# A fused attention, recurrence and expert kernel: WO and the state update change places in TensorE's order

## What is computed

```
# layer 1: gated linear attention, one token after the other
S = exp(gt)[..., None] * S + kt[..., None] * vt[..., None, :]     # state per head
o = einsum('bhk,bhkv->bhv', qt, S)
o = rms(o, rms_w) * (g * sigmoid(g))
x = x + o @ Wo                                                    # output projection
x = x + gelu(ln(x) @ W1 + b1) @ W2 + b2                           # feed-forward
# layers 2 and 4: softmax router, two of eight experts per token
# layer 3: recurrence
h = tanh(xb_t + h @ A.T)                                          # 1024 steps
y = (hs @ C) @ W_out.T + b_out
```

## Time and profile before

| what | value |
|---|---|
| median of three runs | 1946.68 us |
| the profiled execution's own time | 1937.87 us |
| its span, first to last instruction | 1936.1 us |
| mean granted TensorE clock | 0.961 |
| TensorE matmuls busy | 1796.5 us (93%) |
| TensorE weight loads busy | 1553.0 us (80%) |
| VectorE busy | 1310.4 us (68%) |
| POOL busy | 1121.6 us (58%) |
| ScalarE busy | 917.7 us (47%) |
| DMA engines, queue 1 | 7.8% |

### The profile page before, as it was taken

One profiled execution on the slowest core, in us unless ns is written; L12 is line 12 of the kernel. 1 busy time (PEld: TensorE's weight loads), 2 busy tenths in 40 slices (PEclk: granted clock), 3 DMA queues, 4 the chain that ended last, 5 costly groups with the idle time before them and its releaser, 6 DMA issues.

```text
span 1936.1 us, 47586 instructions
## 1 busy us (share of the span) xinstructions
PE 1796.5 (93%) x16264; PEld 1553.0 (80%) x16264; DVE 1310.4 (68%) x3877; ACT 917.7 (47%) x2534; POOL 1121.6 (58%) x1453
## 2 busy tenths in 40 slices
PE   2588899999999999999999999999999999999887
PEld 1467788888888888888888888888888888887765
DVE  2566577777776777777767777777677777765443
ACT  2344455555444545554445455545455554453321
POOL 1666567556666666566667665665675565654211
PEclk9688899999999999999999999999999999999888
DMA  3110000000000000000000000000000000000000
GB/s 115 38 30 23 23 23 19 27 16 27 27 27 22 26 18 27 16 27 27 27 22 22 22 22 22 27 27 27 22 18 25 19 25 28 23 24 4 3 12 11
DMA packets 71883, 47.79 MB, mean 25 GB/s; under 512 B 37616, under 2 KB 71056, under 8 KB 71696
## 3 DMA queue, kind: packets, MB, share of 16 engines
q1 hardware_dynamic: 70368, 45.41, 7.8%
q10 hardware_dynamic: 1456, 1.59, 0.2%
HBM read 30.21 MB, written 16.78 MB: 24 GB/s over the span
## 4 chain that ended last, share of the span: by engine, by line
PE 69%; POOL 17%; ACT 4%; issue 4%; DVE 3%; POOLq 0%; DMA 0%; ACTq 0%; DVEq 0%; SPq 0%
PE ps L956 50%; PE ps L973 8%; POOL sx L434 8%; PE ps L962 3%; PE ps L981 2%; POOL r L348 2%; PE ps L983 2%; POOL osq L430 1%; POOL stage L450 1%; PE ps L1013 1%; PE ps L1018 1%; DVE yT L780 1%; PE ps L993 1%; POOL ra L348 1%; POOL ra L370 1%
## 5 line engine op out<-in xcount | busy, mean ns | idle before, releaser
L956 PE MATMUL ps<-we,yT 128*128 128x512 f32 x3072 | 843.4, 414 | 3.5 <-DVE yT L780 2.2
L956 PEld LDWEIGHTS ps<-we,yT 128*128 128x128 f32 x3072 | 554.5, 193 | 106.2 <-DVE yT L780 7.9
L487 ACT ACTIVATE hs<-ps 16x8 f32<-16x8 f32 x1024 | 177.8, 174 | 836.4 <-PE ps L973 830.0
L973 PEld LDWEIGHTS ps<-hs,aT 128*128 128x128 f32 x2048 | 352.3, 195 | 120.1 <-issue 68.4
L973 PE MATMUL ps<-hs,aT 128*128 128x8 f32 x2048 | 331.4, 236 | 51.8 <-ACT hs L487 50.0
L376 POOL TENSOR_TENSOR part<-part 128x256 f32<-128x256 f32 x64 | 47.4, 741 | 418.1 <-ACT part L505 418.1
L728 DVE SCALAR_TENSOR_TENSOR stage<-ps,coef,stage 128x256 f32<-128x256 f32 x384 | 185.1, 482 | 143.6 <-POOL stage L378 114.7
L434 POOL TENSOR_TENSOR sx<-osq,cst 32x512 f32<-32x512 f32 x128 | 214.8, 1678 | 10.0
L728 DVE SCALAR_TENSOR_TENSOR acc<-ps,coef,acc 128x256 f32<-128x256 f32 x384 | 184.9, 482 | 23.9 <-POOL acc L378 10.5
L399 POOL TENSOR_TENSOR orstd<-omean,mhalf 128x32 f32<-128x32 f32 x32 | 174.1, 5439 | 2.7
L780 DVE TENSOR_TENSOR yT<-ps,yT 128x512 fp32r<-128x512 f32 x64 | 44.0, 691 | 116.6 <-ACT yT L662 67.9
(11 more groups left out here) (172 smaller groups left out, 3504.8 us busy)
## 6 DMA issues: line engine op xcount, KB each, us to landing
xin<-in_x SPq DMA_DIRECT2D x64, 128.0 KB
vrow<-vtok SPq DMA_DIRECT2D x32, 256.0 KB, 2.1
vx<-vrow SPq DMA_DIRECT2D x128, 64.0 KB, 2.0
xag<-in_x SPq DMA_DIRECT2D x64, 128.0 KB
out<-stage SPq DMA_DIRECT2D x64, 128.0 KB
stage<-in_experts SPq DMA_DIRECT2D x1, 2048.0 KB, 7.8
stage<-in_Wvg SPq DMA_DIRECT2D x1, 512.0 KB, 4.2
stage<-in_W SPq DMA_DIRECT2D x1, 512.0 KB, 6.1
```

Source lines behind the costliest of these rows:

```text
L487: return a.activation(hs[0:N, :, k], bt(ps[0:N, BANK["RB"], 0:TOK])[:, :, k], ACT.Tanh)
L956: ins = t.matmul(dst, left(lp, c), right(rp, c), start=(n == 1), stop=(n == 3 * chunks))
L973: return t.matmul(bt(ps[0:NP, BANK["RB"], 0:TOK])[:, :, k], aT[:], hs[:, :, (k - 1) % TS], start=False, stop=True, skip_group_check=True)
```

## The change

Three steps of TensorE's body change their places. `state_update(0)` moves from between steps 3 and 4 of the recurrence to directly behind `scores(0)`. `state_update(1)` moves up one slot, between steps 3 and 4. The output projection WO moves from ahead of step 0 to between steps 4 and 5. Since WO now comes after `DS1`, it counts up a semaphore of its own, `WO`, and VectorE waits for that ahead of `xmid`. Nothing is added or left out of the computation, and the other engines keep their order.

```
@@ vector engine
                 if live(it, 3):
+                    dve.wait_ge(sem("WO"), c3)
                     v.tensor_tensor(xmid[:].rearrange("p i d -> p (i d)"), ps[:, BANK["WO"], :], xhat[:].rearrange("p i d -> p (i d)"), ALU.add).then_inc(sem("xmid"), 1)
@@ tensor engine
                     ins.then_inc(sem("KT"), 1)
-                if live(it, 3):
-
-                    for name, count in readers(it, "WO"):
-                        pe.wait_ge(sem(name), count)
-                    for i in range(TILES):
-                        ins = product(ps[:, BANK["WO"], i * D:(i + 1) * D], lambda p, c: oTs[:, p, c, i * P:(i + 1) * P],
-                                      lambda p, c: wcols(W_O, p, c, D, 0, D), KC)
                 if live(it, 5):
                     recur(0).then_inc(sem("rnn_mm"), 1)
...
                     scores(0)
+                if live(it, 2):
+
+                    target = value(pe, c2)
+                    pe.wait_ge(sem("weights"), WEIGHTS)
+                    pe.wait_ge(sem("ktok"), target)
+                    state_update(0)
...
                     recur(3).then_inc(sem("rnn_mm"), 1)
                 if live(it, 2):
-
-                    target = value(pe, c2)
-                    pe.wait_ge(sem("weights"), WEIGHTS)
-                    pe.wait_ge(sem("ktok"), target)
-                    state_update(0)
+                    state_update(1).then_inc(sem("DS1"), 1)
...
                     recur(4).then_inc(sem("rnn_mm"), 1)
-                if live(it, 2):
-                    state_update(1).then_inc(sem("DS1"), 1)
+                if live(it, 3):
+
+                    for name, count in readers(it, "WO"):
+                        pe.wait_ge(sem(name), count)
+                    for i in range(TILES):
+                        ins = product(ps[:, BANK["WO"], i * D:(i + 1) * D], lambda p, c: oTs[:, p, c, i * P:(i + 1) * P],
+                                      lambda p, c: wcols(W_O, p, c, D, 0, D), KC)
+                    ins.then_inc(sem("WO"), 1)
```

## The result

The changed kernel is slower: the ratio of its runs to those of the kernel before is **1.0047, with a 95% interval from 1.0032 to 1.0063**; the medians of 22 runs each are 1949.78 and 1940.87 us. With more runs the median of before came out at 1940.87 instead of the 1946.68 on which the prediction stood, so 5.8 of the 8.8 us that I called an offset were the draw of three runs. The profiled execution took 1951.02 us (before 1937.87), with a span of 1949.2 us and a granted clock of 0.957. The forecast was 0.27% faster with 42% on "faster" and 16% on "slower"; the sign was wrong.

What follows compares the result with a forecast made beforehand. POOL was taken to bound steps 29 to 7 of each round, leaving TensorE a stall. Terms -8.5 + 3.8 - 0.6 = -5.3 gave 1932.6 us profiled, 1941.4 us as median; range 1930 to 1953, the forecast's own 1937 to 1944.

Steps and rivals of the forecast that it cites:

- the 8.8 us that I called an offset: The median of the runs shown lay 8.8 us above the profiled execution; the forecast kept this, going from 1932.6 to 1941.4 us.
- the clock: TensorE's spells at 1.2 instead of 2.4 GHz: old ones gone, -8.5 us; nine new ones under F2, +3.8 us.
- The last rounds: Last two rounds, where POOL's spreading has ended: 0.1 us gained in one, 0.5 in the other, together -0.6 us.
- What bounds the round: Period of 55.31 us: POOL sets it between recurrence steps 29 and 7, where TensorE has 1.25 us idle.
- TensorE's own sum: TensorE's stretch from the `kt` transposes to step 6: 10.17 instead of 10.25 us, the 0.08 going into the stall.
- Scores directly followed by updates: Change of tiling mode on TensorE between 32-row scores and 32 x 32 updates: no drain price of its own, 1.03 us.
- VectorE's wait for WO: VectorE ahead of `xmid`: WO ends a microsecond before `xmid` is reached, so no cost; 1.18 us of idle as cover.
- the spells behind update 1 go (-8.5): Low-clock spells ahead of the `ym` transposes vanish, as small work behind F2 shrinks from 2.7 to 2.0 us: -8.5 us.
- Others come behind scores 0: Nine new low-clock spells under F2, after 2.9 us of small work where 1.25 stood: 0.42 us each, +3.8 us.
- Rival 3: Low-clock spells come behind step 6, on transposes and routing: 1.5 us each, 1952.6 us at ten spells; chance 14%.
- rival 2: Low-clock spells stay as they are, belonging by the idle-gap rule to the unchanged stall: only -0.6, 1946 us; chance 17%.

## Why the prediction was wrong

- **The sum.** The forecast for the profiled execution was 1932.6 us, and it took 1951.02: 18.4 us more. The collision, priced at nothing, is 5.7 of them, and the clock, priced at +3.8 for new spells and measured at 18.9, is 15.1. The last rounds gained 0.1 us instead of 0.6, and the first rounds, which the sum had left out, gave 2.9 back.
- **What bounds the round** was right: POOL's chain from step 29 to step 7, TensorE from there on. The 0.8 us moved from one part to the other came out as 0.83 a round.
- **TensorE's own sum** (10.25 to 10.17 us, from WO to step 6; "worth: nothing") was right in its verdict. It measured 9.94: the slots of update 0, of F2 and of G2_7 were each 0.08 or 0.09 us shorter than taken. Scores directly followed by updates had no price, as the early round had shown.
- **VectorE's wait for WO, "Cost nothing":** the wait itself, yes. The first failed step is what stands beside it, that VectorE starts "1.6 us earlier" and that "POOL's ops are neither added nor moved". I followed the earlier start only as far as the waits behind it, and never asked which POOL op `y0` would now run beside. The timelines of VectorE and POOL had both times: `y0` stood 1.59 us behind the start of `x2b`, and 1.6 us earlier is exactly on it. Priced at 0, it was 0.29 us in most rounds, 5.7 us in all.
- **The clock, "the spells behind update 1 go (-8.5)":** there was none there in the changed kernel. But the reason given, WO behind update 1, isn't borne out: with only WO moved, ten spells begin right behind the updates, under WO. "Others come behind scores 0": five, not nine, and nearly free, as in such a round `y0` also misses `x2b` (at 446.20, with `x2b` at 1.28). The spells that cost the time came where the sum had none.
- **Rival 3 is what happened**, with 14%: spells behind the stall at 1.5 us each. Measured 13 of them, at 1.45. This is the second failed step, and the larger one. My argument against it, that none had begun there in 26 rounds, held for a stall of 1.25 us; I had put the new one at 1.33 and it became 1.78, of which 0.29 is the collision and the rest TensorE arriving earlier. The missed term and the missed rival are thus linked, and the experiment with `y0` behind `dstate` shows it: without the collision the stall is 1.41 us and the spells behind it are gone. Why the clock falls behind a longer stall stays open.
- **The rule on idle gaps** (rival 2): the Trainium skill, TensorE: Matmul & The Clock Gate, last part, puts drops of clock down to idle gaps between bursts of matmuls, and it speaks of gaps longer than the 1.78 us stall. So none of the spells in the steady rounds is a case of that rule as written, and rival 2 had leaned on it too far. In direction the new spells fit it: they follow the only idle gap, and go when it is shorter. Those behind scores and updates, with TensorE counted busy, don't.
- **The numbers:** the range of 1930 to 1953 held the 1949.78 us, through the end that rival 3 had set; the forecast's own 1937 to 1944 did not. One reading was off a little: the old spells begin 2.4 to 4.4 us ahead of the `ym` transposes, not 2.5 to 4.8. The offset of 8.8 us between three runs and one profiled execution was no property of the kernel; with 22 runs it is 3.

## What to carry to other kernels

When a change makes an engine start earlier, look up not only who waits for it but which ops of other engines it will now run beside. VectorE and POOL can hold each other; if one of the two is on the critical path, let that one start first. A stall on an engine that isn't the bound there costs nothing as such, but here TensorE paid for a longer one afterwards in clock: fill it, best with work from the part where that engine is the bound. And read a small difference from the stretch that the change touches, since the rest of a run can vary by as much. Where two bounds alternate in a round, a gain in the wrong half only lengthens the other's stall.

## What the runs showed of the hardware

- A `tensor_scalar` of 128 x 256 on VectorE and an op of POOL hold each other, and the one that starts second is the longer for it: two of them took 1.16 us instead of 0.73 when `x2b` was first by 0.6 us, and 1.56 when it was first by 0.2; ahead of it, `x2b` took 1.46 instead of 1.28 us and an op on two columns 0.34 to 0.36 instead of 0.19. `att` and `dstate`, which read one operand from PSUM, left `x2b` at 1.27 to 1.30.
- The granted clock fell with the engine counted busy for all of the stretch (4.00 of 4.00 us, clock 0.57), behind work on 32-row tiles and lone steps of 8 columns. With the 12 matmuls of WO ahead of step 0, none of six traces had such a fall behind the first scores in its steady rounds; with WO elsewhere, six traces had two to ten. From the second steady round on, a round with spells was up to 1.8 us longer than a clean one, and some hardly at all, by whether a stall lay behind them.
- The granted clock also fell behind a stall: in one trace twelve times behind stalls of some 1.78 us, at about 1.45 us each. In the same order of TensorE it did so behind none of 1.41 us.
- Scores on 32 x 128 tiles directly followed by updates on 32 x 32 tiles: 1.02 us from start to start, the same as to a full-array step.
